# Expert scatters split into two chains, and the shared expert moved from the pair loop to the change-over

## What is computed

```python
x = _layernorm(x + attention(x))                  # 4096 tokens x 256
scores = sigmoid(x @ gate_w); groups = best 4 of 8; experts = best 6 of 64
# each expert takes at most CAP = 48 of its tokens
h = silu(einsum('ech,ehf->ecf', buf, w_gate)) * einsum('ech,ehf->ecf', buf, w_up)
out = einsum('ecf,efh->ech', h, w_down)           # 64 experts, f = 96
y = segment_sum(gathered * w, tok)                # each expert's rows added to their tokens
shared = silu(x @ ws_gate) * (x @ ws_up) @ ws_down
return _layernorm(x + y + shared)
```

## Time and profile before

| What | us |
|---|---|
| median of 3 runs (1479.05 to 1483.07) | 1482.69 |
| the profiled execution | 1479.91 |
| its span, first to last instruction | 1478.0 |
| PE busy in the span | 1350.9 |
| last attention block of the second last group begins on PE | 1215.23 |
| first transposition of the pair loop on PE | 1258.44 |
| first scatter issued on POOL | 1271.65 |
| last scatter issued on POOL | 1429.32 |
| first load of the final stage issued on SP | 1432.85 |

### The profile page before, as it was taken

One profiled execution on the slowest core, in us unless ns is written; L12 is line 12 of the kernel. 1 busy time (PEld: TensorE's weight loads), 2 busy tenths in 40 slices (PEclk: granted clock), 3 DMA queues, 4 the chain that ended last, 5 costly groups with the idle time before them and its releaser, 6 DMA issues. The chain is left out here.

```text
span 1478.0 us, 36820 instructions
## 1 busy us (share of the span) xinstructions
PE 1350.9 (91%) x13960; PEld 1101.8 (75%) x13960; DVE 899.4 (61%) x2586; ACT 653.6 (44%) x1289; POOL 344.8 (23%) x406
## 2 busy tenths in 40 slices
PE   7999999999999999999999999999999993887820
PEld 5888888888888888888888888888888872554510
DVE  7757575666665656666666666666656574333328
ACT  8644444444444444444444444444444440222204
POOL 0222222122221212121212121212121211444422
PEclk9999999999999999999999999999999995889865
DMA  8810000000000000000000000000000024667538
GB/s 329 308 42 2 23 0 23 0 23 0 23 0 23 0 23 0 23 0 23 0 23 0 23 0 23 0 23 0 23 0 23 0 61 121 173 177 190 132 80 284
DMA packets 57153, 82.09 MB, mean 56 GB/s; under 512 B 4800, under 2 KB 46368, under 8 KB 56224
## 3 DMA queue, kind: packets, MB, share of 16 engines
q1 hardware_dynamic: 51488, 73.42, 15.5%
q0 software_dynamic: 5632, 8.26, 3.1%
HBM read 60.03 MB, written 21.63 MB: 55 GB/s over the span
## 5 line engine op out<-in xcount | busy, mean ns | idle before, releaser
L423 PE MATMUL pB<-sb_xh,sb_W 128*128 (+1 forms) x2048 | 350.4, 273 | 0.6 <-ACT sb_kh L688 0.5
L1109 POOL TENSOR_TENSOR sb_fold<-sb_sq 128x256 f32<-128x256 f32 x128 | 111.7, 873 | 902.7 <-ACT sb_sq L707 902.7
L423 PE MATMUL pB<-sb_xl,sb_W 128*128 (+1 forms) x1024 | 279.7, 273 | 0.0
L423 PEld LDWEIGHTS pB<-sb_xh,sb_W 128*128 128x128 f16 x2048 | 200.6, 98 | 24.8 <-DVE sb_W L794 0.8
L705 ACT ACTIVATE sb_yh<-sb_y 128x512 f16<-128x512 f32 x128 | 80.7, 630 | 289.3 <-DVE sb_y L810 289.3
L499 PE MATMUL pC<-sb_S,sb_v 128*64 128x256 f32 (+1 forms) x2048 | 195.0, 333 | 0.0
L818 DVE TENSOR_TENSOR sb_ql<-sb_q,sb_qh 128x512 f16<-128x512 f32 x128 | 88.0, 688 | 168.6 <-ACT sb_qh L681 165.2
L513 PE MATMUL pO<-sb_Wo,sb_yh 128*128 128x256 f16 x1024 | 176.8, 275 | 5.5 <-DVE sb_yl L814 5.5
L423 PE MATMUL pA<-sb_xh,sb_W 128*128 (+1 forms) x1024 | 175.9, 274 | 5.6 <-DVE sb_W L794 5.6
L680 ACT ACTIVATE sb_q<-pA 128x512 f32<-128x512 f32 x128 | 76.5, 597 | 231.7 <-PE pA L423 231.7
L423 PE MATMUL pA<-sb_W,sb_xh 128*128 128x256 f16 x1024 | 175.9, 274 | 1.7 <-ACT sb_qh L681 1.7
(11 more groups left out here) (166 smaller groups left out, 2276.7 us busy)
## 6 DMA issues: line engine op xcount, KB each, us to landing
sb_D<-w_experts SPq DMA_DIRECT2D x24, 384.0 KB, 3.7
sb_stage<-wprep SPq DMA_DIRECT2D x7, 1280.0 KB, 6.5
sums<-sb_zeros SPq DMA_DIRECT2D x2, 4096.0 KB, 24.0
gather_rows<-sb_xr SPq DMA_DIRECT2D x16, 320.0 KB, 2.3
sb_D<-w_down SPq DMA_DIRECT2D x24, 192.0 KB, 4.3
sb_xs<-xT SPq DMA_DIRECT2D x17, 256.0 KB, 2.8
sb_D<-decay SPq DMA_DIRECT2D x8, 512.0 KB, 7.6
sb_xn<-x SPq DMA_DIRECT2D x16, 256.0 KB, 2.9
```

Source lines behind the costliest of these rows:

```text
L423: last = nc.tensor.matmul(dst, a, m, start=(i == 0), stop=(i == len(terms) - 1), **kw)
L1109: nc.gpsimd.tensor_tensor(fold[:, :], sq[:, 0:T], sq[:, T:2 * T], ALU.add).then_inc(s_fold, 1)
```

## The change

1. **Scatters.** Each expert's 48 rows are scattered alone, from its own buffer on partitions 0 to 47. Even experts form one chain into region 0, odd ones another into region 1 (`s_sc[0]`, `s_sc[1]`). There are 64 scatters in place of 32. Each is issued with an index column straight from `sidx` and `gidx`; the copies of single columns on DVE (`gcol`, `scol`) go.
2. **Regions.** They are no longer filled with zeros. Region 1 starts with the normed tokens (SP stores them per sequence, `store_x1`), region 0 with the shared expert's rows, stored whole in the change-over. The final stage adds two regions and no third part; its chunks are now one DMA for both regions in pieces of 2 KB, and ACT issues the stores.
3. **Shared expert.** It is computed in 16 units of 256 tokens in the change-over, between the last sequence's routing pieces on PE (`unit_gate_up`, 12 matmuls in f16 high and low parts; `unit_down`, 2 in f32). ACT takes Silu and a copy, POOL multiplies (units 0 to 11) or DVE (12 to 15), and ACT empties the result and issues its store. Its input is the transposed tokens in f16 high and low parts, which each sequence now makes (one more activation on ACT, one subtraction on DVE) and stores to `x1_split`; SP loads 15 units back at the end.
4. **Pair loop.** No shared part. It is written out 32 times, with no loop. SP holds weights of 16 pairs (`RING`) and loads them all before the loop; pairs 16 to 31 follow as pairs 0 to 15 are done.

```diff
-RING = 8
+RING = 16
+XRING = 8
...
+        TAIL = ["g0 g1", "d0 g2 d1 g3 d2 g4 d3", "", "d4", "g5 g6 d5 g7 d6 d7", "", "g8 g9 d8 g10 d9 g11 d10", "",
+                "d11 g12 g13 d12 d13 g14 g15 d14 d15"]
+        BY_POOL = 12
...
-            for i in range(2):
-                sp.dma_start(sums[TOK * i:TOK * (i + 1), :].rearrange("(p k) n -> p (k n)", p=P).rearrange("p (r m) -> p r m", m=HID),
-                             zeros[:, :].unsqueeze(1).broadcast_to([P, TOK // P, HID])).then_inc(s_zero, 16)
...
+            def store_x1(b):
+                sp.wait_ge(s_x1, b)
+                sp.dma_start(x1_t[bass.ds(b - 1, 1)].rearrange("o p t n -> (o p) t n"), xr[:, :, 0:HID]).then_inc(s_x1r, 16)
...
+                store_x1(b)
+                store_split(b)
                 store_rows(b)
...
+            sp.wait_ge(s_x1s, 16 * SEQS)
+            for j in range(UNIT_EARLY):
+                load_unit(j)
             sp.wait_ge(s_g, STEPS)
-            for r in range(in_d, RING):
+            for j in range(UNIT_EARLY, SEQS - 1):
+                load_unit(j)
+            for r in range(in_w):
                 load_pair(r, r)
...
+            sp.wait_ge(s_D, STEPS)
+            for r in range(in_w + in_d, RING):
+                load_pair(r, r)
+            store_x1(SEQS)
             store_rows(SEQS)
...
+            for p in range(RING, PAIRS):
+                sp.wait_ge(s_md, p - RING + 1)
+                load_pair(p, p % RING)
...
+            def unit_gate_up(j):
...
+                wait(pe, s_uact, j - 1)
+                for s in range(2):
+                    last = group(pGU[j % 2][0:FF, s * T:(s + 1) * T],
+                                 [((wshh, wshl)[w][:, c, s * FF:(s + 1) * FF], units[j][:, t, c, :])
+                                  for c in range(NC) for w, t in PASSES])
+                last.then_inc(s_ugu, 1)
+
+            def unit_down(j):
+                pe.wait_ge(s_ush, j + 1)
+                wait(pe, s_uev, j - 1)
+                for t in range(NT):
+                    last = group(pUD[j % 2][:, t * HID:(t + 1) * HID], [(us[0:FF, j % 2, t * P:(t + 1) * P], wsd[:, :])])
+                last.then_inc(s_udn, 1)
...
-                for c in range(NC):
-                    nc.tensor.transpose(pT[r % 2][:, SH + c * P:SH + (c + 1) * P], x1s[:, r, c * P:(c + 1) * P], ident[:, :])
...
-                for s in range(2):
-                    last = group(pH[r % 2][0:FF, SH + s * P:SH + (s + 1) * P],
-                                 [(wsh[:, c, s * FF:(s + 1) * FF], sxT[:, r % 2, c, :]) for c in range(NC)])
...
-                nc.tensor.matmul(pDn[r % 2][:, SH:SH + HID], sh[:, r % OUTBUF, :], wsd[:, :], start=True, stop=True)
...
+            pe.wait_ge(s_uact, SEQS)
+            pe.wait_ge(s_uev, SEQS)
+            transpose_tokens(0)
...
+            def unit_store(j):
+                act.wait_ge(s_udn, j + 1)
+                wait(act, s_ust[j % UEV], 16 * (j // UEV))
+                nc.scalar.activation(ue[j % UEV], pUD[j % 2][:, :], ACT.Copy).then_inc(s_uev, 1)
+                act.wait_ge(s_uev, j + 1)
+                act.dma_start(shared_t[j], ue[j % UEV].rearrange("p (t n) -> p t n", t=NT)).then_inc(s_ust[j % UEV], 16)
...
-                    nc.vector.tensor_tensor(f0[c], f0[c], f1[c], ALU.add).then_inc(s_fadd, 1)
+                    nc.vector.tensor_tensor(fin[c][:, 0, :, :], fin[c][:, 0, :, :], fin[c][:, 1, :, :], ALU.add).then_inc(s_fadd, 1)
...
-                if c < FINALS:
-                    dve.wait_ge(s_fadd, 2 * c + 1)
-                    nc.vector.tensor_tensor(f0[c], f0[c], fo[c], ALU.add).then_inc(s_fadd, 1)
...
+            def scatter(p, e):
+                pool.wait_ge(s_wo, p + 1)
+                wait(pool, s_sc[e], 16 * p)
+                nc.gpsimd.indirect_dma_start(sums[:, :], bass.IndirectOffsetOnAxis(ap=sidx[:, 2 * p + e:2 * p + e + 1], axis=0),
+                                             wo[:, 2 * (p % OUTBUF) + e, :], None, compute_op=ALU.add).then_inc(s_sc[e], 16)
```

More of the change, by code:

```diff
@@ L231, in block_kernel @@
[L231 to L237 removed]
+        late = 2 * in_w * PAIR_W
+        units = [xe[:, j, :] for j in range(UNIT_EARLY)]
@@ L554, in step @@
                 g = b * NQ + q
-                if isinstance(b, int) and b == SEQS and q >= 2:
+                tail = isinstance(b, int) and b == SEQS
+                if tail and q >= 2:
                     piece(b, q, STEPS)
+                    if q == 2:
+                        unit_down(4)
+                    if q == 3:
+                        for u in "g5 g6 d5 g7 d6 d7".split():
+                            unit(u)
+                    if q == 5:
+                        for u in "g8 g9 d8 g10 d9 g11 d10".split():
+                            unit(u)
                     return
@@ L565, in step @@
                     attention((q - 2) % NQ, g - 2)
+                if tail:
+                    for u in ("g0 g1", "d0 g2")[q].split():
+                        unit(u)
                 if has(g):
@@ L572, in step @@
                     piece(b, q, g - 1)
+                if tail and q == 1:
+                    for u in "d1 g3 d2 g4 d3".split():
+                        unit(u)
                 if isinstance(b, int) and b == 0 and q == NQ - 1:
@@ L739, in step @@
                     act_gate(q, g)
+                if isinstance(b, int) and b == 0 and q == NQ - 1:
+                    act.wait_ge(s_const, 16 * 7)
+                    nc.scalar.activation(wshh[:, :, :], wsh[:, :, :], ACT.Copy, scale=W_SCALE).then_inc(s_wshh, 1)
+                if isinstance(b, int) and b == SEQS:
+                    for u in TAIL[q].split():
+                        unit(u)
             act.wait_ge(s_xin, 16)
```

371 lines of the change are left out of this document (195 added, 176 removed).

## The result

The changed kernel takes 1471.8 us (median of 5 runs, 1468.64 to 1473.76) where the kernel before takes 1482.69: a ratio of 0.9931, with a 95% interval from 0.9911 to 0.9951. It is faster by 10.9 us and not by the 35.7 of the forecast. The profiled execution took 1473.76 us, its span is 1471.9. The other 4.8 us between the medians are traced nowhere.

A forecast was written before the change was run, and what follows sets the result against it. It took the chain of scatters to set the pair loop's time, PE to bound attention and DVE the final stage. +3.4 (change-over) - 36.5 (loop) + 0.2 (last pair) - 2.8 (final) is -35.7: median 1447 us, range 1430 to 1473.

The forecast's parts named there:

- What bounds the kernel now: Whole kernel: PE bounds attention, the routing chain the change-over, the chain of scatters the pair loop, DVE the final stage.
- Attention, 0 us: Attention: dropping the zero fill gains nothing and the added activation, subtraction and stores stay hidden, 0 us.
- Change-over, 3.4 us later: Change-over: with the shared expert's units on PE, the first scatter comes 3.4 us later, at 1275.
- through when the rows are ready, or a few us later; the units still hide that: Change-over: the last rows' store, queued on SP behind 16 pairs and 11 units, needs 40 us and delays nothing.
- the start at low clock goes: Loop start: PE's first transpositions no longer run slow, part of 4.7 us less from first transposition to first scatter.
- The rival of late rows: Change-over: last rows' store and units are late, gathers start 10 us later, 1457 us in all; chance 0.09.
- Pair loop, 36.5 us less: Pair loop: the 31 links from first to last pair take 121.2 us for 157.7; the heading says 35 less.
- the issue of a 48-row scatter: Pair loop, POOL: issue taken as 0.95 us, in the middle of 0.63 and 1.48, nearest to the gather's.
- the longer of two things: Pair loop: a pair takes the longer of the chain, 3.3 us (4.3 with weights' traffic), and POOL itself, 3.75.
- The wait of 2.33: Pair loop: waiting for a scatter's landing falls from 2.85 us to 2.33, losing packet time alone.
- Last pair and final stage, 2.6 us less: End: the last pair's second scatter adds 0.2 us, the final stage, bound by the DMAs, saves 2.8.
- the fixed price of a scatter: Pair loop: a scatter costs the same whatever its rows, POOL bounds at 4.8 us a pair, 1472 us; chance 0.20.

The follow-up runs named there:

- the two cures tried: Changed kernel with the last rows' store ahead of the weights of pairs 8 to 15: 1472.28 us; with those weights also behind the units' stores: 1478.05 us.

## Why the prediction was off

**What bounds the kernel now: right.** One chain sets the loop's pace at 4.4 us, and traffic adds to it: the run with one chain has 4.41 and, beside the weights, 5.18. The run without weight loads shows the traffic's part in the changed kernel by itself. What the part left out is the end, where POOL's drain and not the last store closes the program.

**Attention, 0 us: held, as far as traces tell.** The profile of after is 2.5 us late from the start-up on, with no growth behind it (the block of the earlier trace rows at 1217.69 for 1215.23). Ten other traces of kernels with the same attention have it at 1215.46 to 1216.68, 1216.07 in the mean, and the one with the attention of before has 1215.90. So most of the 2.5 is how the first loads fell in one execution. A change of the attention by half a us could not be told from it.

**Change-over, 3.4 us later: 5.4.** PE's work, clock and end were right: full clock, and the units end 1.6 us earlier than forecast once the late start is taken off (1267.36 - 2.46 = 1264.9 for 1266.5). The step that failed is "through when the rows are ready, or a few us later; the units still hide that". The store was issued at 1253.7 and took about 12 us to land, so the first gather came at 1266.3 (10.69 us of waiting for it); PE then waited 2.35 and 1.74 us. A second step failed with it: "the start at low clock goes". As PE waited, its first two transpositions took 0.61 and 0.63 us, as at the old start (0.66), and from the first of them to the first scatter it took 9.8 us and not 8.5. So PE came 0.7 late and the scatter another 1.3, the 2.0 in all. The rival of late rows happened in part, and neither of the two cures tried gained anything.

**Pair loop, 36.5 us less (35 in the part's heading): 12.4.** This is the step that broke the forecast, by 24.1 us, and the term is the issue of a 48-row scatter: taken as 0.95, measured as 1.35. I had made the 0.53 us by which a scatter's issue exceeds a gather's a cost per row and let both share the rest. The runs show the reverse: the rows cost 0.13 us from 48 to 112 and 0.07 from 16 to 48, the accumulation 0.46 in a scatter of 48. The observation that a gather moves more bytes per row and is still cheaper stood in the text as an argument for the rival; it should have decided.

Put into the forecast's own sum, 1.35 gives 13 x 4.68 + 13 x 4.55 + 5 x 3.68, 138.4 us, so this term is 17.2 of the 24.1. The other 6.9 lie in the loaded pairs: 14 of them took 5.20, for the 4.68 that the sum then gives to 13. The traffic is what does it, since without the weights they take 4.58. How it does it is argued and not shown: the sum took "the longer of two things" with fixed lengths, and where both are near 4.6 and one varies, a late landing adds a wait and an early one gives nothing back. The rows fit that, with pairs from 4.57 to 6.06 and none below. The other terms were good: the wait of 2.33 (a pair of the tail takes 3.66, less 1.33 of issue), the gap of 0.30, POOL as the bound, PE at the low clock without harm.

**Last pair and final stage, 2.6 us less: 1.6.** The rest of the stage did better than forecast: from the last scatter it takes 3.6 us less, although the drain took 2.6 more, so without it 6.2. The DMAs gave 397 GB/s from 1440 to 1460 for the 353 of the earlier trace rows and the 380 taken:

```profile
1440.00:1460.00 20.00, 0.00 (x0) 0.00 (x0) 18.02 (x77) 11.52 (x22) 7.07 (x11) 0.50 1.05 397
```

and DVE, busy 18 of these 20 us, is still the bound for the most part, and not the DMAs as forecast. A chunk without waits takes it 1.68 us (1438.37 to 1440.05), not 1.46; from 1452 on it waits for loads before most chunks, by 0.25 to 0.62. The second scatter of the last pair came 2.0 us behind the first, for 1.25.

**The rivals.** What happened is the first, the fixed price of a scatter, with part of the second. It had 1472 as its time and a chance of 0.20. That 1472 is so close is in part luck: its loop of 146 us was 26 equal pairs of 4.81, with a price of 1.48, where the run has 14 of 5.20 and 11 of 4.58 with a price of 1.35. The argument against it, that the longer issue "must come from something that it does per row", was an argument from how one thinks that it works and had no row behind it.

**Where the gain of 10.9 us is from.** Not from the split, which alone in the old kernel gives a ratio of 0.9987. Without it, the rest of the change is at 0.9894: the shared expert's work moved beside the routing costs some 3.6 us of change-over (first scatter 1276.23 for 1271.65, less 1.0 of start-up), and frees the loop of traffic and of copies (147.0 for 157.7) and the end of an addition (43.2 for 48.7).

## What to carry to other kernels

Price an indirect DMA by its count first: before you split one, add up the issues on its engine, and take the nearest row's whole duration as the likely price of a smaller one (here 1.48 for what measured 1.35, against a guess of 0.95). If a chain of accumulating DMAs is the bound, let whole ones alternate between two places rather than cut each in two, and pay with memory and with a longer sum at the end. When two resources are nearly equal in length and one of them varies, expect a pace slower than either. And before you move a store ahead in a queue, look when its data are ready: what stands behind it waits too, and the DMAs may run empty.

## What the runs showed of the hardware

- An accumulating scatter has POOL busy for 1.28, 1.35 and 1.48 us for 16, 48 and 112 rows of 1 KB; writing 48 without accumulation takes 0.89, gathering 112 rows of 1.25 KB 0.93 to 0.98 (1.19 the first). The least gap between two of them is 0.30.
- POOL's closing drain takes 6.05 us behind 64 indirect DMAs and 8.66 behind 96 (with scatters of 16 or of 48 rows), and 0.80 when an earlier drain has done this work. It can be what ends a program: 3.5 us behind SP's closing drain (1468.2), which waits for the last store, in the changed kernel.
- PE at 1.2 GHz, busy all of a stretch of 60 us by the profile (60.00), didn't get its full clock; with ten more small matmuls per pair, it had 1.00 and was busy 52.05. The Trainium skill ("Perfetto Trace Analysis", the most contended engine) warns that the busy share of matmuls is a bad measure of how close PE is to its peak; its "TensorE: Matmul & The Clock Gate", part 1, says that activity releases the clock. The two stretches agree with the first. With the second only the stretch at 1.00 does; the other shows the low clock at the higher busy share, so this share alone doesn't tell whether the clock will be full.
- The first loads of a kernel fall differently from one execution to the next: a block 1.2 ms later began within 2.2 us (1215.46 to 1217.69) in eleven traces with the same attention ahead of it (three of them also fill two regions with zeros at the start).
